# Fused local attention on one core: masks on POOL alone, head sums in one product, late weights in parts, arguments behind projections

## Chip, cores and metric

The kernel runs on one core of a Trainium2 chip. The metric is the device time of one execution in microseconds; less is better.

## What is computed

Two transformer-like layers of three blocks each on x, which is (4, 1024, 512) in float32: a gated linear state space block, cross attention and a stack of linears with tanh; then local attention, cross attention on gathered keys and a gated feed-forward block with FP4 quantisation. A layer norm stands behind each block. The change touches the fourth block, local attention:

```python
g = x @ Wg.T + bg; v = x @ Wv.T + bv             # 16 heads of 32
dot = einsum('bhid,bhjd->bhij', g, g)
nrm = norm(g, axis=-1)
corr = dot / (nrm[..., :, None] * nrm[..., None, :] + 1e-08)
m = (j <= i) & (j >= i - 128)
corr = (corr * m + 1.0) / 2.0
denom = mean(corr, axis=3) + 0.5
fitness = 1.0 / (denom * sum(1.0 / denom, axis=2))
weighted = corr * fitness[..., None]
attn = softmax(weighted * m + (1.0 - m) * NEG)   # NEG = -1e10
out = einsum('bhij,bhjd->bhid', attn, v) @ Wo.T + bo
```

Each query sees itself and the 128 keys before it.

## The kernel before

The program is a row of stages: preparation, the state space block with the products of weights, cross attention with the linears, `local_attention` (L1146), and a last stage for the two remaining attentions' outputs and the feed-forward block. Stages don't overlap.

`local_attention` runs over 4 batches times 4 chunks of 4 heads (16 chunks) times 8 tiles of 128 keys, 128 tiles in all, two per round. A loop over `ROUNDS` is written once per engine, and its order is the order of each engine's queue; semaphores join them. In round s, with p = s + 12 and x = s - 2, the engines work on three ages of tiles at once, held in a ring of 16 buffers `TR`:

- For tiles p and p+1, TensorE makes the arguments (`arguments`, L1426: the two banks 4 and 5, so the arguments of one tile wait until tanh of the tile before has read them), ScalarE takes tanh (L1607), and POOL masks it (`mask_tanh`: L1376 for the keys' own tile of queries, L1381 for the next tile of queries). One round later `gather` (L1432, L1446, L1453) sums tanh over keys with the tiles `GN`.
- Per chunk and half, `sums` (L1525) adds over each head's 32 rows with the block matrix `BO`: four products, each 128 x 32 by 512 columns. ScalarE (`denominator`, `fourth_power`) and VectorE (`inverse`, `share`, `scaled`: L1741 to L1761) make the fitness `GS` of it. In rounds with `sums` the first arguments stand behind the gathers and wait for `denominator` (L1619), which frees bank 4.
- For tiles s and s+1, TensorE makes the scores (`dots`, L1472) in banks 0 to 3, VectorE combines them with the tanh tile (L1714), ScalarE takes the exponential in place (L1612), and POOL masks it (`mask_exp`).
- For tiles x and x+1, `attend` sums values (L1483) and weights (L1486) in bank `PVS`. `mask_exp` masks the own tile only. The unseen corner of the next tile is not zero after the exponential but 1 (its tanh was set to -1, so its exponent is 0), and `unseen` (L1495) takes it back by a product of the values with `UM`, which holds -1 in that corner; the count of it is taken from the sums by the constants `begin` and `begin1`, with which `start_bank` opens the bank.

Beside this the same rounds project the input for batches to come: tile m = p // 4 + 10, in part 0 (here called a g round) the transposes of x (L1537) and the product for g (L1543), in part 1 (a v round) the transposes of unit rows (L1551) and the product for v (L1556). The projections use banks 0 to 3 as well. ScalarE's copies L1641 (x), L1651 (unit rows) and L1656 (v), and VectorE's L1782 (g), empty them; `dots` waits for all of these (L1465 to L1469), and `projections` waits until VectorE has used both scores of its round (L1530). The last projected tile is m = 31, in the rounds up to p = 86; 38 rounds have both scores and a projection. At a batch's end a g round also holds the logarithms (L1662), eight small VectorE steps (L1804 to L1816), and the following v round the transposes L1566 and the copies L1668.

On ScalarE a round is: the square of g, the denominators, tanh(p), exp(s), exp(s+1), tanh(p+1), then the copies of the projection, then `normaliser` (L1636). On TensorE the order at the end of a round is (L1593 to L1599):

```python
if there(x):
    attend(x)
if there(p):
    arguments(p + 1)
projections(*projected(p), s)
if there(x):
    attend(x + 1)
```

SyncE issues the loads of `GN` (L1319), `GT`, `VN` (L1339) and the stores. Once the last tile is projected (p == 98), `weights_after_projections` (L1285) loads the weights of the next stage in one round: `VB`, `Wo` and the feed-forward's down weights, whose four transfers (L1294) go to 32 partitions each.

Of the kernel before, what the change touches and what calls it, by code (L numbers as in the profile page):

```python
# [8 lines left out]
BF16 = mybir.dt.bfloat16  # L9
# [4 lines left out]
P = 128  # L14
B = 4
# [1130 lines left out]
def local_attention(k):  # L1146
# [12 lines left out]
    with ExitStack() as ctx:  # L1159
# [27 lines left out]

        begin, begin1, empty = (sb(n, [P, D], BF16) for n in ("begin", "begin1", "empty"))
# [3 lines left out]
        S0, CR, MC, UM = sb("S0", [P, WIN]), sb("CR", [P, WIN]), sb("MC", [P, P]), sb("UM", [P, P])  # L1192
# [3 lines left out]
        s_zero, s_one, s_bo, s_mc, s_um, s_cm, s_cr, s_con, s_begin = (sem(n) for n in (  # L1196
            "zero", "ones", "block_ones", "causal", "unseen", "count_mm", "count", "constants", "begin"))
# [27 lines left out]
        with k.nc.Block() as block:  # L1225
            @block.sync
            def _(e):
# [57 lines left out]
                def weights_after_projections():  # L1285

                    for s in (s_v, s_gh, s_s2, s_gt):
                        e.wait_ge(s.sem, s.at(NT))
# [14 lines left out]
                for s in ROUNDS:  # L1303
# [39 lines left out]
                e.wait_ge(s_next.sem, s_next.at(32))  # L1343
# [4 lines left out]
            def _(e):  # L1348
# [4 lines left out]
                for t in (begin, begin1, empty):  # L1353
                    e.memset(t[:, :], 0.0).then_inc(s_begin.sem, 1)

                e.memset(MC[:, :], 1.0).then_inc(s_mc.sem, 1)
                e.memset(UM[:, :], -1.0).then_inc(s_um.sem, 1)
# [3 lines left out]
                e.wait_ge(s_um.sem, s_um.at(1))  # L1361
                e.affine_select(out=UM[:, :], in_=UM[:, :], compare_op=ALU.is_ge, fill=0.0, base=-1,
                                pattern=[[1, P]], channel_multiplier=-1).then_inc(s_um.sem, 1)
# [28 lines left out]

# [8 lines left out]
                for s in ROUNDS:  # L1401
# [4 lines left out]
                    if there(s):  # L1406
                        mask_exp(s)
                        mask_exp(s + 1)
# [938 lines left out]
```

## Time and profile before

| | |
|---|---|
| median of 3 runs | 2823.32 us (2823.13 to 2826.96) |
| the profiled execution | 2823.76 us |
| its span, first to last instruction | 2822.0 us |
| mean granted TensorE clock | 0.976 |
| busy: TensorE, VectorE, ScalarE, POOL | 2649.0, 1911.6, 807.9, 799.6 us |
| local attention with scores | about 1057 to 1623 us |
| the last stage | about 1626 to 2822 us |

A row of the timeline gives start, duration, engine, line, operation, the tiles written and read and their shapes, how many instructions were merged, and in brackets the idle time of that engine before them with what ended it. The duration of merged products includes the tail of the last one; how long a group holds TensorE is read from its start to the start of the next. PE is TensorE, ACT is ScalarE, DVE is VectorE, SP is SyncE.

### The profile page before, as it was taken

To read this page: it belongs to the slowest core of one execution; us is meant where nothing else is said; L and a number is where in the kernel's file an instruction comes from. 1 tells how busy PE (TensorE), PEld (TensorE's weight loads), DVE (VectorE), ACT (ScalarE), POOL (GpSimd) and SP (SyncE) were. 2 spreads that over 40 slices of the span, in tenths; PEclk is the share of its full clock that TensorE was granted. 3 is DMA by queue.
4 is the path that set the end of the run, shared out by engine and by line. 5 is a ranking of instruction groups with operands and counts; after the bars stand their busy time and mean duration, and the time that the engine had idled before them with its cause. 6 is when DMAs were issued, how large, how long until landed. Compare 5 with 4: busy or idle time off the path is not lost. (4 is left out here: it accounts for less than half of the span.)

```text
span 2822.0 us, 38888 instructions
## 1 busy us (share of the span) xinstructions
PE 2649.0 (94%) x14094; PEld 1608.6 (57%) x14094; DVE 1911.6 (68%) x3307; ACT 807.9 (29%) x1193; POOL 799.6 (28%) x794
## 2 busy tenths in 40 slices
PE   7999988999998889999997869999999999999996
PEld 3444535555555444555554536777777777777774
DVE  3688403666667336666676748888888888888884
ACT  1111313333332246656576611111111111111110
POOL 1233103555544345554554411111111111111000
PEclk9999989999999999999998979999999999999998
DMA  5344130000000233333335411111111111111111
GB/s 163 120 161 167 60 114 1 1 1 1 1 1 1 65 101 92 91 95 96 94 98 137 147 34 40 43 43 43 43 43 44 43 43 43 43 43 43 40 39 33
DMA packets 219322, 177.04 MB, mean 63 GB/s; under 512 B 38239, under 2 KB 184031, under 8 KB 218110
## 3 DMA queue, kind: packets, MB, share of 16 engines
q1 hardware_dynamic: 182150, 147.85, 17.6%
q10 hardware_dynamic: 36984, 26.71, 3.5%
q8 instruction: 115, 1.88, 0.3%
q14 instruction: 73, 0.60, 0.1%
HBM read 90.51 MB, written 52.43 MB: 51 GB/s over the span
## 5 line engine op out<-in xcount | busy, mean ns | idle before, releaser
L2032 PE MATMUL bank<-tiles,tl_XQT 128*128 128x512 f32 (+1 forms) x768 | 331.3, 575 | 8.6 <-DMA tl_XQT<-tl_QB 5.7
L2047 PE MATMUL bank<-tiles,tl_HT 128*128 128x512 f32 x704 | 317.8, 607 | 19.8 <-DMA tl_HT<-tl_tmp 19.8
L2037 PE MATMUL bank<-tiles,tl_XQT 128*128 128x512 f32 (+1 forms) x768 | 318.0, 557 | 0.0
L2047 PEld LDWEIGHTS bank<-tiles,tl_HT 128*128 128x128 f32 x704 | 225.3, 325 | 96.7 <-issue 29.8
L2032 PEld LDWEIGHTS bank<-tiles,tl_XQT 128*128 128x128 f32 x768 | 232.6, 311 | 74.4 <-issue 16.0
L2037 PEld LDWEIGHTS bank<-tiles,tl_XQT 128*128 128x128 f32 x768 | 236.8, 308 | 65.4
L1376 POOL TENSOR_SCALAR_AFFINE_SELECT tiles<-tiles 128x512 f32<-128x512 f32 x256 | 175.8, 699 | 289.8 <-ACT tiles L1607 259.1
L1985 POOL TENSOR_TENSOR tl_rs<-tl_ve,mhalf 128x1 f32<-128x1 f32 x32 | 17.6, 550 | 594.4 <-DVE tl_ve L2140 594.4
L2081 ACT ACTIVATE tl_HQ<-bank 128x512 f32<-128x512 f32 (+1 forms) x96 | 53.9, 562 | 426.9 <-PE bank L2032 405.5
L1714 DVE SCALAR_TENSOR_TENSOR tiles<-tiles,bank 128x1024 f32<-128x1024 f32 (+1 forms) x128 | 141.8, 1149 | 28.2 <-PE bank L1472 28.0
L1977 POOL TENSOR_TENSOR tl_rs<-tl_ve,mhalf 128x1 f32<-128x1 f32 x32 | 19.9, 622 | 426.0 <-DVE tl_ve L2122 426.0
L1607 ACT ACTIVATE tiles<-bank 128x1024 f32<-128x1024 f32 (+1 forms) x128 | 123.5, 965 | 45.5 <-PE bank L1426 45.4
L1612 ACT ACTIVATE tiles<-tiles 128x1024 f32<-128x1024 f32 (+1 forms) x128 | 124.9, 1000 | 20.0 <-DVE tiles L1714 17.0
L1993 PE MATMUL bank<-home_T,tl_AT 128*128 128x512 f32 x256 | 121.9, 621 | 6.5 <-DMA tl_AT<-attended 6.5
L2115 DVE TENSOR_TENSOR X<-bank,X 128x512 f32<-128x512 f32 x32 | 22.1, 692 | 152.0 <-PE bank L2047 152.0
L960 PE MATMUL bank<-space_T 128*128 128x512 f32 x256 | 121.0, 617 | 2.3 <-DVE X L1108 2.3
L2075 ACT ACTIVATE tl_XT<-bank 128x512 f32<-128x512 f32 x32 | 19.1, 598 | 347.5 <-PE bank L2000 332.6
L1543 PE MATMUL bank<-home_T,tiles 128*128 128x512 f32 x256 | 117.1, 601 | 0.0
L1556 PE MATMUL bank<-home_odd,tiles 128*128 128x512 f32 x256 | 116.7, 599 | 0.0
L1005 PE MATMUL bank<-space_T,space_quant 128*128 128x512 f32 x256 | 115.2, 593 | 1.5 <-ACT space_quant L1062 1.5
L995 PE MATMUL bank<-space_even,space_quant 128*128 128x512 f32 x256 | 115.3, 593 | 1.2 <-ACT space_quant L1057 1.1
L1399 POOL TENSOR_TENSOR la_rn<-la_n,mhalf 128x16 f32<-128x16 f32 x32 | 92.7, 2897 | 50.1 <-DVE la_n L1789 50.1
(289 smaller groups left out, 5025.4 us busy)
## 6 DMA issues: line engine op xcount, KB each, us to landing
tl_HT<-tl_tmp SPq DMA_DIRECT2D x256, 44.0 KB, 2.0
tl_HT<-tl_tmp ACTq DMA_DIRECT2D x256, 44.0 KB, 2.0
fp_weights<-space_quant ACTq DMA_DIRECT2D x33, 256.0 KB, 2.2
X<-in_x SPq DMA_DIRECT2D x8, 1024.0 KB, 11.8
v<-tiles SPq DMA_DIRECT2D x32, 256.0 KB, 2.4
unit_g<-tiles SPq DMA_DIRECT2D x32, 256.0 KB, 2.4
unit_gT<-tiles SPq DMA_DIRECT2D x32, 256.0 KB, 2.8
la_GN<-unit_g SPq DMA_DIRECT2D x128, 64.0 KB, 2.0
```

The source lines that it names most:

```text
L960: mm = e.matmul(bank[turn(s, 0)][:, :], WqT[:, c, m * P:(m + 1) * P], XT[g % 2][:, c, :], start=(c == 0), stop=(c == C - 1))
L995: mm = e.matmul(bank[turn(s, 1)][:, :], AT[:, c, :], WoT[:, c, :], start=(c == 0), stop=(c == C - 1))
L1376: return e.affine_select(out=x[:, :, 0:P], in_=x[:, :, 0:P], compare_op=ALU.is_ge, fill=fill, base=0, pattern=[[0, HC], [1, P]], channel_m ...
L1543: mm = e.matmul(bank[1][:, :], XT[m % 2][:, c, :], WgT[:, c, :], start=(c == 0), stop=(c == C - 1))
L1556: mm = e.matmul(bank[2][:, :], XT[m % 2][:, c, :], WvT[:, c, :], start=(c == 0), stop=(c == C - 1))
L1607: e.activation(TR[p % RING][:, :, 0:cols(t)], four(ARG[:, :])[:, :, 0:cols(t)], ACT.Tanh).then_inc(s_T.sem, 1)
L1612: e.activation(y, y, ACT.Exp).then_inc(s_p.sem, 1)
L1714: e.scalar_tensor_tensor(out=y, in0=y, scalar=1.0, in1=d, op0=ALU.add, op1=ALU.mult).then_inc(s_u.sem, 1)
L1993: mm = e.matmul(bank[LOUT][:, :], AT[n % 2][:, c, :], WoT[:, c, :], start=(c == 0), stop=(c == C - 1))
L2032: mm = e.matmul(bank[(2 * q) % 3][:, 0:w], chunk(XQT[n % 2], c), WgT[q][:, :, c, :], start=(c == 0), stop=(c == C - 1))
L2037: mm = e.matmul(bank[(2 * q + 1) % 3][:, 0:w], chunk(XQT[n % 2], c), WuT[q][:, :, c, :], start=(c == 0), stop=(c == C - 1))
L2047: mm = e.matmul(bank[DOWN][:, :], chunk(HT, q), WdT[:, q, :], start=(q == 0), stop=(q == IC - 1))
```

## The change

1. `mask_exp` masks both halves of the exponentials, as `mask_tanh` does. `unseen`, `UM`, `begin` and `begin1` go; `start_bank` always uses the zeros of `empty`. On POOL the second exponential's mask moves behind the second tanh's.
2. `sums` is one product of 128 x 128 by 512 columns.
3. `weights_after_projections` is called in eleven consecutive rounds, from p = 98 to 118: the down weights in eight parts of 6 or 5 slices to 32 partitions, then `VB`, then `Wo` in two halves.
4. On TensorE `projections` stands ahead of `arguments(p + 1)`.

```diff
+                def weights_after_projections(i):
+
+                    if i == 0:
+                        for s in (s_v, s_gh, s_s2, s_gt):
+                            e.wait_ge(s.sem, s.at(NT))
                     VB, WoT = k.out_weights
-                    e.dma_start(VB, k.SW[:, VO_AT:FOLDED]).then_inc(s_next.sem, 16)
-                    e.dma_start(WoT[:, :, :], chunked(a["L1_attn_Wo_T"])).then_inc(s_next.sem, 16)
-
-                    for j in range(4):
-                        e.dma_start(k.tiles[32 * j:32 * j + 32, DOWN_AT:DOWN_AT + IC * D].rearrange("p (i d) -> p i d", d=D),
-                                    down_rows[32 * IC * j:32 * IC * (j + 1), :].rearrange("(i p) d -> p i d", p=32)).then_inc(k.d_wd, 16)
+                    if i < 8:
+
+                        j, q = i // 2, (0, 6, IC)[i % 2:i % 2 + 2]
+                        at = DOWN_AT + q[0] * D
+                        e.dma_start(k.tiles[32 * j:32 * j + 32, at:at + (q[1] - q[0]) * D].rearrange("p (i d) -> p i d", d=D),
+                                    down_rows[32 * (IC * j + q[0]):32 * (IC * j + q[1]), :].rearrange("(i p) d -> p i d", p=32)).then_inc(k.d_wd, 16)
+                    elif i == 8:
+                        e.dma_start(VB, k.SW[:, VO_AT:FOLDED]).then_inc(s_next.sem, 16)
+                    elif i < 11:
+                        c = 2 * (i - 9)
+                        e.dma_start(WoT[:, c:c + 2, :], chunked(a["L1_attn_Wo_T"])[:, c:c + 2, :]).then_inc(s_next.sem, 16)
...
-                    if p == C * G * (B - 1) + 2:
-                        weights_after_projections()
+                    if p >= C * G * (B - 1) + 2:
+                        weights_after_projections((p - C * G * (B - 1) - 2) // 2)
...
                 def mask_exp(x):
-
                     e.wait_ge(s_p.sem, s_p.at(x + 1))
-                    own_tile(TR[x % RING], 0.0).then_inc(s_pm.sem, 1)
+                    i = own_tile(TR[x % RING], 0.0)
+                    if x % G < G - 1:
+                        i = next_tile(TR[x % RING], 0.0)
+                    i.then_inc(s_pm.sem, 1)
...
                     if there(s):
                         mask_exp(s)
-                        mask_exp(s + 1)
                     if there(p):
                         mask_tanh(p + 1)
+                    if there(s):
+                        mask_exp(s + 1)
...
-                        mm = start_bank(PVS, begin if t else begin1)
+                        mm = start_bank(PVS)
                         if t == 0 and x:
                             mm.then_inc(s_pv.sem, 1)
                         if t:
-                            unseen(x - 1)
                             values(x - 1, P, P).then_inc(s_pv.sem, 1)
...
                     if t % 2 == 0:
-                        unseen(x)
                         values(x, 0, WIN).then_inc(s_pv.sem, 1)
...
-                    for h in range(HC):
-                        q = slice(DH * h, DH * h + DH)
-                        mm = e.matmul(bank[4][q, :], BO[:, q], ZZ[:, half_of(r)], start=True, stop=True)
-                    mm.then_inc(s_S.sem, 1)
+                    e.matmul(bank[4][:, :], BO[:, :], ZZ[:, half_of(r)], start=True, stop=True).then_inc(s_S.sem, 1)
...
                     if there(x):
                         attend(x)
+                    projections(*projected(p), s)
                     if there(p):
                         arguments(p + 1)
-                    projections(*projected(p), s)
                     if there(x):
                         attend(x + 1)
```

TensorE before, from the first arguments of a v round to the next scores:

```order
L1426 MATMUL bank<-la_RR,la_LR 128x512 x2
L1432 MATMUL bank<-la_begin,la_ones 32x512 x4
L1495 MATMUL bank<-la_UM,la_VN 32x128 x4
L1483 MATMUL bank<-tiles,la_VN 32x128 x4
L1486 MATMUL bank<-tiles,ones 32x128 x4
L1495 MATMUL bank<-la_UM,la_VN 32x128 x4
L1483 MATMUL bank<-tiles,la_VN 32x256 x4
L1486 MATMUL bank<-tiles,ones 32x256 x4
L1426 MATMUL bank<-la_RR,la_LR 128x512 x2
L1551 MATMUL bank<-ident,tiles 128x128 x4
L1556 MATMUL bank<-home_odd,tiles 128x512 x4
L1483 MATMUL bank<-tiles,la_VN 32x128 x4
```

TensorE now, the same piece (L1429 is what L1426 was, L1435 was L1432, L1486 and L1489 were L1483 and L1486, L1539 and L1544 were L1551 and L1556):

```order
L1429 MATMUL bank<-la_RR,la_LR 128x512 x2
L1435 MATMUL bank<-la_empty,la_ones 32x512 x4
L1486 MATMUL bank<-tiles,la_VN 32x128 x4
L1489 MATMUL bank<-tiles,ones 32x128 x4
L1486 MATMUL bank<-tiles,la_VN 32x256 x4
L1489 MATMUL bank<-tiles,ones 32x256 x4
L1539 MATMUL bank<-ident,tiles 128x128 x4
L1544 MATMUL bank<-home_odd,tiles 128x512 x4
L1429 MATMUL bank<-la_RR,la_LR 128x512 x2
L1486 MATMUL bank<-tiles,la_VN 32x128 x4
```

The two products against `UM` are gone, and the second pair of argument products stands behind the projection.

SyncE before, where the late weights are issued:

```order
L1231 DMA la_VN<-v 128x128 x2
L1290 DMA home_odd<-folded 128x1536
L1291 DMA home_T<-in_L_attn_Wo_T 128x4x512
L1294 DMA tiles<-fp_weights 32x11x512 x4
L1231 DMA la_GN<-unit_g 128x128 x2
```

SyncE now, from the first part on:

```order
L1230 DMA la_VN<-v 128x128 x2
L1294 DMA tiles<-fp_weights 32x6x512
L1230 DMA la_GN<-unit_g 128x128 x2
L1336 DMA attended<-la_AO 128x256
L1230 DMA la_VN<-v 128x128 x2
L1294 DMA tiles<-fp_weights 32x5x512
```

Each part stands behind the `VN` tiles of its round and ahead of the next round's `GN` tiles.

## Rows read from the trace of the kernel before

**Rows 1.** The stretch with projections and scores: busy time by engine, clock, DMA

```profile
1057.00:1444.00 387.00, 364.23 (x4420) 192.90 (x4420) 248.43 (x466) 237.69 (x330) 204.79 (x237) 1.00 0.33 93
```

**Rows 2.** Timeline of TensorE and ScalarE in a v round

```profile
1250.53 1.06 PE L1525 MATMUL bank<-la_ZZ,la_BO 128*32 128x512 f32 x8
1251.42 0.40 PE L1432 MATMUL bank<-la_empty,la_ones 128*32 128x512 bf16 x4
...
1253.44 0.39 PE L1495 MATMUL bank<-la_UM,la_VN 128*32 128x128 f32 x8
1253.66 0.39 PE L1483 MATMUL bank<-tiles,la_VN 128*32 128x128 f32 x8
...
1255.28 0.39 PE L1426 MATMUL bank<-la_RR,la_LR 32*128 32x512 bf16 x2
1255.60 0.66 PE L1551 MATMUL bank<-ident,tiles 128*128 128x128 f32 x4
1256.09 3.60 PE L1556 MATMUL bank<-home_odd,tiles 128*128 128x512 f32 x8
1259.62 0.43 PE L1483 MATMUL bank<-tiles,la_VN 128*32 128x128 f32 x8
1259.73 0.60 ACT L1656 ACTIVATE tiles<-bank 128x512 f32<-128x512 f32 x1 [2.50 <-PE bank L1556]
1260.69 1.15 PE L1472 MATMUL bank<-la_GS,la_GT 32*128 32x256 f32 x16 [0.42 <-ACT tiles L1656]
```

**Rows 3.** Timeline before the first scores: arguments, tanh, the copy behind it

```profile
1021.29 0.39 PE L1426 MATMUL bank<-la_RR,la_LR 32*128 32x512 bf16 x2 [0.85 <-ACT tiles L1607]
1021.72 1.02 ACT L1607 ACTIVATE tiles<-bank 128x1024 f32<-128x1024 f32 x1 [0.48 <-PE bank L1426]
1022.64 0.59 ACT L1651 ACTIVATE tiles<-bank 128x512 f32<-128x512 f32 x1
```

**Rows 4.** Timeline of a g round's end, then a v round with a narrow second tile

```profile
1269.05 0.16 PEld L1483 LDWEIGHTS bank<-tiles,la_VN 128*32 128x32 f32 x8 [0.76 <-issue]
1270.16 1.15 PE L1472 MATMUL bank<-la_GS,la_GT 32*128 32x256 f32 x16 [0.47 <-issue]
...
1276.85 0.59 ACT L1607 ACTIVATE tiles<-bank 128x512 f32<-128x512 f32 x1
...
1280.63 1.15 PE L1472 MATMUL bank<-la_GS,la_GT 32*128 32x256 f32 x16 [0.42 <-ACT tiles L1656]
```

**Rows 5.** Timeline of the following g round, with the logarithms of a batch

```profile
1286.27 0.59 ACT L1641 ACTIVATE tiles<-bank 128x512 f32<-128x512 f32 x1
...
1288.17 0.31 ACT L1662 ACTIVATE la_ln<-la_nc 128x128 f32<-128x128 f32 x1
...
1291.18 0.94 PE L1472 MATMUL bank<-la_GS,la_GT 32*128 32x256 f32 x16 [1.53 <-issue]
```

**Rows 6.** Late weights: DMA issues (KB each, us to landing), TensorE's wait, scores of every fourth round

```profile
tiles<-fp_weights SPq DMA_DIRECT2D x4, 704.0 KB, 16.3
...
1483.82 1.15 PE L1472 MATMUL bank<-la_GS,la_GT 32*128 32x256 f32 x16 [0.65 <-DVE la_GS L1761]
...
1507.08 1.08 PE L1453 MATMUL bank<-tiles,la_GN 128*32 128x256 f32 x8 [15.29 <-DMA la_GN<-unit_g]
...
1524.90 1.15 PE L1472 MATMUL bank<-la_GS,la_GT 32*128 32x256 f32 x16 [0.65 <-DVE la_GS L1761]
...
1549.07 1.15 PE L1472 MATMUL bank<-la_GS,la_GT 32*128 32x256 f32 x16 [0.65 <-DVE la_GS L1761]
```

**Rows 7.** Behind the projections: second tanh, head sums; POOL's selects, ns min/median/max

```profile
1553.63 1.00 ACT L1607 ACTIVATE tiles<-bank 128x1024 f32<-128x1024 f32 x1
...
1555.10 1.06 PE L1525 MATMUL bank<-la_ZZ,la_BO 128*32 128x512 f32 x8
...
L1376 POOL TENSOR_SCALAR_AFFINE_SELECT tiles<-tiles x256: 628/634/1130, 1014.6 to 1615.0; 128x512 f32<-128x512 f32 x128
```

**Rows 8.** Timeline of TensorE near the stage's end: scores after a gap

```profile
1596.29 1.62 PE L1472 MATMUL bank<-la_GS,la_GT 32*128 32x256 f32 x16 [2.44 <-DVE la_GS L1761]
```

More of the change, by code:

```diff
@@ L1185, in local_attention @@
         ones16 = sb("ones16", [P, DH], BF16)
-        begin, begin1, empty = (sb(n, [P, D], BF16) for n in ("begin", "begin1", "empty"))
+        empty = sb("empty", [P, D], BF16)
         ZZ, UU = sb("ZZ", [P, T]), sb("UU", [P, D])
@@ L1191, in local_attention @@
         SQ = [sb(f"SQ{n}", [P, WIN]) for n in range(2)]
-        S0, CR, MC, UM = sb("S0", [P, WIN]), sb("CR", [P, WIN]), sb("MC", [P, P]), sb("UM", [P, P])
+        S0, CR, MC = sb("S0", [P, WIN]), sb("CR", [P, WIN]), sb("MC", [P, P])
         BO, half = sb("BO", [P, P]), sb("half", [P, 1])
@@ L1195, in local_attention @@
         S2, S, S4, rS = sb("S2", [P, 2]), sb("S", [P, 1]), sb("S4", [P, 1]), sb("rS", [P, 1])
-        s_zero, s_one, s_bo, s_mc, s_um, s_cm, s_cr, s_con, s_begin = (sem(n) for n in (
-            "zero", "ones", "block_ones", "causal", "unseen", "count_mm", "count", "constants", "begin"))
+        s_zero, s_one, s_bo, s_mc, s_cm, s_cr, s_con, s_begin = (sem(n) for n in (
+            "zero", "ones", "block_ones", "causal", "count_mm", "count", "constants", "begin"))
         d_row = [sem(f"load_rows{n}") for n in range(2)]
@@ L1352, in _ @@
                 e.memset(ones16[:, :], 1.0).then_inc(s_begin.sem, 1)
-                for t in (begin, begin1, empty):
-                    e.memset(t[:, :], 0.0).then_inc(s_begin.sem, 1)
+                e.memset(empty[:, :], 0.0).then_inc(s_begin.sem, 1)
                 e.memset(MC[:, :], 1.0).then_inc(s_mc.sem, 1)
-                e.memset(UM[:, :], -1.0).then_inc(s_um.sem, 1)
                 e.wait_ge(s_mc.sem, s_mc.at(1))
@@ L1428, in arguments, with start_bank @@
                     mm.then_inc(s_arg.sem, 1)
-                def start_bank(n, src):
+                def start_bank(n):
                     for h in range(HC):
-                        mm = e.matmul(bank[n][DH * h:DH * h + DH, :], ones16[:, :], src[:, :], start=True, stop=False)
+                        mm = e.matmul(bank[n][DH * h:DH * h + DH, :], ones16[:, :], empty[:, :], start=True, stop=False)
                     return mm
@@ L1438, in gather @@
                         e.wait_ge(s_z.sem, s_z.at(2 * n))
-                        start_bank(WB, empty)
+                        start_bank(WB)
                     if t == HG:
                         e.wait_ge(s_z.sem, s_z.at(2 * n + 1))
-                        start_bank(WB, empty)
+                        start_bank(WB)
                         for h in range(HC):
@@ L1488, in values @@
                     return mm
-                def unseen(x):
-                    c = ((x + 1) % 2) * P
-                    for h in range(HC):
-                        q = slice(DH * h, DH * h + DH)
-                        e.matmul(bank[PVS][q, c:c + P], VN[x % TILES][:, q], UM[:, :], start=False, stop=False)
                 def attend(x):
@@ L1522, in sums @@
                         e.wait_ge(s_bo.sem, s_bo.at(3))
-                    for h in range(HC):
-                        q = slice(DH * h, DH * h + DH)
-                        mm = e.matmul(bank[4][q, :], BO[:, q], ZZ[:, half_of(r)], start=True, stop=True)
-                    mm.then_inc(s_S.sem, 1)
+                    e.matmul(bank[4][:, :], BO[:, :], ZZ[:, half_of(r)], start=True, stop=True).then_inc(s_S.sem, 1)
                 def projections(m, part, s):
@@ L1821, in constants @@
                     e.reciprocal(MC[:, :], bank[PVS][:, 0:P]).then_inc(s_con.sem, 1)
-                    e.wait_ge(s_begin.sem, s_begin.at(4))
-                    e.tensor_scalar(begin[0:1, WIN:WIN + P], bank[PVS][0:1, 0:P], 1.0, -1.0, ALU.subtract, ALU.mult)
-                    e.tensor_scalar(begin[0:1, WIN + P:2 * WIN], bank[PVS][0:1, 0:P], 1.0, -1.0, ALU.subtract, ALU.mult).then_inc(s_begin.sem, 1)
-                    e.tensor_scalar(begin1[0:1, WIN + P:2 * WIN], bank[PVS][0:1, 0:P], 1.0, -1.0, ALU.subtract, ALU.mult).then_inc(s_begin.sem, 1)
                     e.wait_ge(s_con.sem, s_con.at(2))
@@ L2042, in down @@
                     if n == 0:
-                        e.wait_ge(k.d_wd, 64)
+                        e.wait_ge(k.d_wd, 128)
                     e.wait_ge(s_a6.sem, s_a6.at(n))
```

11 lines of the change are left out of this document (1 added, 10 removed).

## Prediction

> **What bounds the kernel now.** I first read the page's slices: TensorE is busy 9 tenths or more nearly throughout, except in the slices around 1440 to 1620 us, inside local attention. The chain of waits starts behind this stage and says nothing of it, so I went by stretches. From 1057 to 1444 us, while projections run beside attention, TensorE is busy 364 of 387 us at full clock [rows 1]. A microsecond of TensorE is there a microsecond of the kernel, unless somebody else takes over. Then I read the timeline of single rounds, to see which wait ends last in each.
>
> One round handles two tiles. In the projection stretch two kinds alternate. A **v round** ends with the product of values; its block of L1556 is over where L1483 starts, at 1259.62. Behind it ScalarE copies the bank (L1656), and TensorE's next scores (L1472) start 1.07 us after the product's end, and 0.96 us after the copy's start [rows 2]. So the copy already binds: the scores want the bank that the copy empties. A **g round** ends the same way, 1.11 us from product to scores [rows 4]. The tanh of the second tile is done long before, since its arguments (L1426) stand ahead of the projection [rows 2].
>
> Behind the projections four rounds take 24.17 us (1524.90 to 1549.07), but the four in which the late weights load take 41.08 (1483.82 to 1524.90) [rows 6]. In them L1294 puts four transfers of 704 KB, which land 16.3 us later, into the one queue that also carries the GN tiles, and TensorE stands still for 15.29 us until such a tile arrives.
>
> The profiled execution took 2823.76 us, its span is 2822.0, the median of three runs 2823.32. The sum is made against 2823.8, which is 0.4 us above that median.
>
> **Part 1: the arguments behind the projections.** This is the dearest part, and it is a loss. ScalarE's order is not changed: tanh(p), two exponentials, tanh(p+1), then the copies of the projection. The diff puts arguments(p+1) on TensorE behind the projection, so tanh(p+1) starts only then, and the copies wait behind it on ScalarE. With T the end of the projection product, rows of the time before the first scores give each step: arguments to tanh 0.43, tanh to the copy behind it 0.92 [rows 3]. In a v round there follow the copy of unit rows, about 0.50 (an estimate: it is 0.59 long, and the tanh of 1.02 was followed after 0.92), and 0.96 from L1656 to the scores [rows 2]. Scores at T + 2.81, where they were at T + 1.07: 1.74 later. T itself is earlier by the arguments that left (0.32, from 1255.28 to 1255.60) and by two products against UM that the other part removes (0.22 each, 1253.44 to 1253.66; together 0.43). Net **+0.99 us**. In every second v round the second tile is half as wide: its tanh takes 0.59 instead of 1.02 [rows 4], only one UM product stands there (0.22) and the arguments are half as long (0.21), so +0.88. In a g round the copy of x stands directly behind the tanh: 0.43 + 0.92 + 0.59 + 0.36 = 2.30 against 1.11 [rows 3, 4], less 0.75: **+0.44**.
>
> 38 rounds have a projection and scores, 19 of each kind. Two g rounds also hold the logarithms, whose table load and eight small VectorE steps come behind the copy of x: 1.90 us from that copy to the logarithm and 3.01 from there to the next scores [rows 5]. Now these run beside the product; behind it, the scores come at T + 6.26. T is 8.36 − 0.75 = 7.61 us into the round [rows 2, 4], so 13.87 us instead of 10.55 (1280.63 to 1291.18) [rows 4, 5]: +3.3 each. Two v rounds hold two more copies of 0.5 behind the product: +1.5 each. Sum: 17 × 0.44 + 2 × 3.3 + 7 × 0.99 + 10 × 0.88 + 2 × 1.5 = 32.8. The six rounds before the first scores: tanh(p+1) now holds up the next arguments instead of tanh(p) the second; +0.4 each at most, 2 in all. The 5 us gaps of the two logarithm rounds should cost clock: after a gap of 2.44 us the same scores took 1.62 us where they take 1.15 [rows 8]. I take 1.5 us each, 3. Part 1 with the UM products of these rounds: **+38**.
>
> What is behind the waiting scores: the two steps scores(s), scores(s+1) on VectorE, then the exponentials; all shift with them and none was the bound of these rounds. On POOL the mask of tanh(p+1) and the inverse norm come later too, but the inverse norm is wanted only late in the next round.
>
> **Part 2: masks on POOL, UM products gone.** 112 groups of products go, 0.22 us each, 24 us of TensorE. In projection rounds they are counted above. In the 26 rounds behind them they are worth little: of four rounds (24.17 us) only in the first does TensorE hold the others up. Its second tanh starts 4.56 us in and ends at about 5.58, the head sums that need its bank start at 6.03 [rows 7]: 0.4 us can be won, the rest of the four rounds hangs on tanh, exponentials and the fitness chain. 6.5 × 0.41 = **−2.7**. POOL takes 112 selects more; the median of one is 0.63, the longest 1.13 [rows 7]. A round then has up to eight of them, 5.1 of 6.0 us, and their results are wanted one round later. I cost that at nothing; the cover is this microsecond. SBUF — State Buffer, section "SBUF: two separate sides", in the Trainium skill, says that a VectorE operation with two SBUF inputs and a reading GpSimd operation exclude each other for the whole instruction, whichever starts first. The spread of the selects agrees. By that rule the fitness chain, which binds one late round in four, could lose up to a select's length each time, an estimate of some 4 us in all.
>
> **Part 3: head sums in one product.** Four narrow products of 512 columns took 0.89 us together (1250.53 to 1251.42) [rows 2]. One full product of 512 columns takes a quarter of the L1556 block, (1259.62 − 1256.09) / 4 = 0.88 [rows 2]. So nothing is won. TensorEngine Tiling, section "Key Properties", in the Trainium skill, says that a change of tiling mode drains the array, and one more change stands here; by an estimate from that rule the part would lose in each of its 32 uses. The rows show a change of shape from L1426 to L1551 at about 0.1 (0.32 for a product of 0.21). I take 0.07 × 32 = **+2**; bounds 0 and +6.
>
> **Part 4: late weights in parts.** Four rounds of 41.08 against 24.16: the stall with its slow clock costs 16.9 us. A part is 0.4 MB (VB 0.8, a half of Wo 0.5) behind the VN tiles of its round. 2.8 MB landed in 16.3 us [rows 6], so a part takes about 2.3 us, VB 4.5. The next GN tiles are issued some 3 us later, and have another 3 in hand. **−16.9**; if every part still held up its round by 1 us, −6.
>
> The zeroed and filled constants at the start lie under the first projections: 0.
>
> **Sum:** +38 + 2 − 2.7 − 16.9 = +20.4. **Predicted 2844 us.**
>
> **Rivals.** *All gains real, no new wait.* If tanh(p+1) did not hold the scores, because ScalarE's copies were done within 1.82 us of T (the 1.07 of now and the 0.75 that T wins), the projection rounds would gain 0.43 each: −8 to −16 there, −19.6 behind, about 2790. For it: TensorE now waits for tanh(p) in some rounds. Against it: 2.81 us of fixed steps stand in ScalarE's queue, a full microsecond too many. It decides at 1.82. Chance 0.07, and 0.12 for a cheaper form, in which half of the loss is hidden: about 2827.
>
> *Clock lost in every v round.* The new gap ahead of the scores is about 1.8 us. Gaps of 1.53 [rows 5] left the scores' speed alone, one of 2.44 did not [rows 8]. If 1.8 is enough, each of 19 rounds loses up to 1.7: +30, 2874. Chance 0.1.
>
> *POOL becomes the bound.* If selects stretch beside VectorE to 0.9 us on average, between median and longest, eight take 7.2 us against rounds of 6.0. The gathers wait for the tanh masks from 0.75 us a select on; +0.5 to 1 in 26 rounds gives 2857 to 2870. The median speaks against it. Chance 0.1.
>
> My own case has 0.61.
>
> **How the numbers follow.** A measurement can tell 0.2%, 5.6 us, from no change. Faster than that: the first rival and a few of its cheaper form, 0.1. Within it: most of the cheaper form, 0.1. Slower: 0.8. The forecast alone spans 2836 to 2854 (half or one and a half of the logarithm rounds and of the stall's relief). The range must take in the POOL case and the near edge of the cheaper form: 2826 to 2870.
>
> **What would show it.** Right: scores (L1472 of before) wait for ScalarE's copies by about 1.8 us in v and 1.3 in g rounds, tanh has an idle time of some 4 us ahead of its second tile, a cycle of four projection rounds lasts 43.1 instead of 40.4, and the logarithm rounds nearly 14. The wait for GN is gone, and four rounds behind the projections take 23.8. Wrong: projection rounds under 9.5 us, a DMA wait of several us at the new parts, POOL without idle time, or slow products in the v rounds.

## The result, and the profile after

| | before | after |
|---|---|---|
| median | 2823.38 us of 4 runs (2823.13 to 2826.96) | 2858.48 us of 4 runs (2856.91 to 2858.99) |
| profiled execution, its span | 2823.76, 2822.0 us | 2858.96, 2857.2 us |
| mean granted TensorE clock | 0.976 | 0.971 |

The ratio is 1.012 (95% interval 1.0103 to 1.0138): slower, by 35 us. 2844 was forecast, with 2826 to 2870 as the range. The direction and the range hold; the size is 14.5 us short. One of the fifteen runs of the kernel before in the second group of experiments took 8473.08 us, for a reason that isn't known, and no ratio below uses it.

The changed lines keep their form and have new numbers: the scores L1475 (was 1472), arguments L1429 (1426), tanh L1595 (1607), the copies L1629 (x, was 1641), L1639 (unit rows, 1651), L1644 (v, 1656) and L1656 (YT, 1668), the v product L1544 (1556), the head sums L1514 (1525), `scores` on VectorE L1702 (1714).

I begin with the same stretch of time as in [rows 1]. The columns are stretch, length, busy time of TensorE, its weight loads, VectorE, ScalarE, POOL, then granted clock and DMA.

```profile
1057.00:1444.00 387.00, 327.82 (x3313) 166.66 (x3313) 218.30 (x409) 206.79 (x290) 209.38 (x266) 0.94 0.29 81
```

TensorE was busy 364 of these 387 us at full clock; now it is busy 328, with a clock of 0.94. Both losses that follow are in this one line: it waits, and it runs slower. (The stretch is the same, the work in it is not: fewer rounds fit.) POOL's busy time rose only from 204.8 to 209.4, though it masks more in each round.

The end of a full v round in the timeline of TensorE and ScalarE, with the head sums at its start, answers to [rows 2]:

```profile
1277.08 1.12 PE L1514 MATMUL bank<-la_ZZ,la_BO 128*128 128x512 f32 x2
1278.14 0.40 PE L1435 MATMUL bank<-la_empty,la_ones 128*32 128x512 bf16 x4
...
1281.92 3.60 PE L1544 MATMUL bank<-home_odd,tiles 128*128 128x512 f32 x8
1285.45 0.39 PE L1429 MATMUL bank<-la_RR,la_LR 32*128 32x512 bf16 x2
1285.88 1.02 ACT L1595 ACTIVATE tiles<-bank 128x1024 f32<-128x1024 f32 x1 [3.49 <-PE bank L1429]
1286.80 0.59 ACT L1639 ACTIVATE tiles<-bank 128x512 f32<-128x512 f32 x1
1287.28 0.60 ACT L1644 ACTIVATE tiles<-bank 128x512 f32<-128x512 f32 x1
1288.24 1.15 PE L1475 MATMUL bank<-la_GS,la_GT 32*128 32x256 f32 x16 [1.83 <-ACT tiles L1644]
```

The product ends at 1285.45 (T). The arguments follow it, tanh starts 0.43 later, the copy of unit rows 0.92 after that, the copy of v another 0.48, and the scores 0.96 behind its start: T + 2.79, where 2.81 was worked out. The scores wait 1.83 us for the copy.

The next two microseconds were not in the forecast's sum. The same stretch by windows of 2 us, columns as above:

```profile
1286.00:1288.00 2.00, 0.41 (x16) 0.14 (x8) 0.00 (x0) 2.00 (x4) 0.95 (x2) 1.00 0.11 33
1288.00:1290.00 2.00, 1.76 (x24) 1.09 (x28) 0.98 (x2) 0.57 (x2) 2.00 (x3) 0.85 0.59 166
1290.00:1292.00 2.00, 2.00 (x36) 1.43 (x32) 2.00 (x3) 1.92 (x3) 2.00 (x2) 0.50 0.40 113
1292.00:1294.00 2.00, 2.00 (x29) 1.18 (x22) 2.00 (x6) 0.89 (x1) 2.00 (x4) 0.79 0.36 114
```

The granted clock falls to 0.50, which is 1.2 instead of 2.4 GHz, and is back after some 3 us. All products in between take longer: the g round that follows lasts 11.38 us (1288.24 to 1299.62). The g round behind a narrow v round, whose wait is 1.40, lasts 9.68 (1266.54 to 1276.22); before, the two kinds took 9.47 and 9.37. The wait of 1.83 comes seven times in this execution, and the g round behind it loses time each time: six take 11.4 us, and the seventh, which has less to project, takes 10.06 with a clock of 0.50 in its third and fourth microsecond. But the wait ahead of the very first scores, 2.40 us, and the next one, 1.76, left the clock at 1.00.

Next the waits between 1057 and 1660 us (total, times, longest):

```profile
POOL tiles L1376 <- ACT tiles L1595: 231.9, 85, 10.4
ACT tiles L1595 <- PE bank L1429: 175.9, 68, 5.5
...
PE bank L1475 <- ACT tiles L1644: 29.3, 18, 2.4
...
PE bank L1475 <- ACT tiles L1629: 18.8, 16, 1.8
...
PE bank L1475 <- issue: 11.3, 3, 5.5
...
PE bank L1475 <- ACT la_YT L1656: 7.2, 3, 2.6
```

ScalarE waits for arguments 68 times. TensorE waits for ScalarE's copies ahead of the scores, 55 us by the lines on L1644, L1629 and L1656 together, and 11 more in the logarithm rounds ("issue"). POOL itself waits for tanh, as a follower would; whether it is one the first experiment decides.

A logarithm round and the v round behind it in the timeline, answering to [rows 5]:

```profile
1131.27 0.39 PE L1429 MATMUL bank<-la_RR,la_LR 32*128 32x512 bf16 x2
1131.70 1.02 ACT L1595 ACTIVATE tiles<-bank 128x1024 f32<-128x1024 f32 x1 [3.41 <-PE bank L1429]
1132.62 0.59 ACT L1629 ACTIVATE tiles<-bank 128x512 f32<-128x512 f32 x1
...
1134.52 0.31 ACT L1650 ACTIVATE la_ln<-la_nc 128x128 f32<-128x128 f32 x1
...
1137.77 1.66 PE L1475 MATMUL bank<-la_GS,la_GT 32*128 32x256 f32 x16 [5.54 <-issue]
...
1153.53 2.09 PE L1475 MATMUL bank<-la_GS,la_GT 32*128 32x256 f32 x16 [2.55 <-ACT la_YT L1656]
```

The copy, the logarithm and VectorE's small steps now begin behind the product. The scores, at 1123.63 a round earlier, come at 1137.77 after 5.54 us of idle TensorE: the round takes 14.14 (13.87 was worked out). The next scores come at 1153.53, 15.76 us later, partly at half clock; and behind their own wait of 2.55 us the next g round takes 12.73 us, again partly at half clock.

Behind the projections the late weights (DMA issues: number, KB each, us to landing) and the scores of every fourth round answer to [rows 6]:

```profile
tiles<-fp_weights SPq DMA_DIRECT2D x4, 384.0 KB, 4.5
...
tiles<-fp_weights SPq DMA_DIRECT2D x4, 320.0 KB, 4.0
```

```profile
1539.44 1.15 PE L1475 MATMUL bank<-la_GS,la_GT 32*128 32x256 f32 x16 [1.09 <-DVE la_GS L1749]
...
1563.48 1.15 PE L1475 MATMUL bank<-la_GS,la_GT 32*128 32x256 f32 x16 [1.09 <-DVE la_GS L1749]
```

No GN tile is waited for; the four rounds with the first parts take 24.03 us (1515.41 to 1539.44) and the next four 24.04.

So the spans of the profiled executions differ by 35.2 us as follows: +0.9 up to the first scores; +54.8 in the 40 rounds behind them (1057.16 to 1459.68 before, 1058.06 to 1515.41 now: 402.5 and 457.35 us); −17.1 in eight late rounds (65.22 against 48.07); +0.5 in the rest of the scores; −3.9 behind the last scores, which start at 1610.88 and 1649.95. That last piece lies between 1207 and 1212 us in the kernels of this study, whatever they change, and I ascribe it to no edit.

### The profile page after: what moved, and what is told of

It is laid out like the page before. It is cut to its first block and busy times, and to the rows that moved or that the text cites. A ratio compares the mean times of both kernels' runs of the same rounds, so it can differ in the third digit from the quotient of the medians.

```text
span 2857.2 us, 36840 instructions
## 1 busy us (share of the span) xinstructions
PE 2648.9 (93%) x13006; PEld 1592.8 (56%) x13006; DVE 1915.8 (67%) x3304; ACT 806.0 (28%) x1193; POOL 859.7 (30%) x902
## 5 line engine op out<-in xcount | busy, mean ns | idle before, releaser
L1376 POOL TENSOR_SCALAR_AFFINE_SELECT tiles<-tiles 128x512 f32<-128x512 f32 x256 | 174.4, 684 | 268.8 <-ACT tiles L1595 252.9
L1595 ACT ACTIVATE tiles<-bank 128x1024 f32<-128x1024 f32 (+1 forms) x128 | 124.1, 969 | 199.6 <-PE bank L1429 198.9
L1702 DVE SCALAR_TENSOR_TENSOR tiles<-tiles,bank 128x1024 f32<-128x1024 f32 (+1 forms) x128 | 141.8, 1149 | 34.7 <-PE bank L1475 34.5
L1381 POOL TENSOR_SCALAR_AFFINE_SELECT tiles<-tiles 128x512 f32<-128x512 f32 x224 | 151.6, 677 | 0.0
L1475 PE MATMUL bank<-la_GS,la_GT 32*128 32x256 f32 (+1 forms) x1024 | 74.5, 406 | 74.1 <-ACT tiles L1644 29.3
L1600 ACT ACTIVATE tiles<-tiles 128x1024 f32<-128x1024 f32 (+1 forms) x128 | 124.8, 1000 | 19.0 <-DVE tiles L1702 15.9
```

Of the source, the lines that this page charges most:

```text
L1376: return e.affine_select(out=x[:, :, 0:P], in_=x[:, :, 0:P], compare_op=ALU.is_ge, fill=fill, base=0, pattern=[[0, HC], [1, P]], channel_m ...
L1381: return e.affine_select(out=x[:, :, P:WIN], in_=x[:, :, P:WIN], compare_op=ALU.is_ge, fill=fill, base=0, pattern=[[0, HC], [-1, P]], chan ...
L1595: e.activation(TR[p % RING][:, :, 0:cols(t)], four(ARG[:, :])[:, :, 0:cols(t)], ACT.Tanh).then_inc(s_T.sem, 1)
L1600: e.activation(y, y, ACT.Exp).then_inc(s_p.sem, 1)
L1702: e.scalar_tensor_tensor(out=y, in0=y, scalar=1.0, in1=d, op0=ALU.add, op1=ALU.mult).then_inc(s_u.sem, 1)
```

## The experiments

Theory A: the order on TensorE makes tanh(p+1), and behind it the copies, late. Theory B: the masks on POOL cost the time. Theory C, an addition to A: the wait of 1.83 us takes the clock. Each kernel is compared with runs of the kernel before on the same chip, whose medians were 2823.39, 2822.79 and 2823.40 us in the three groups. Stretches given as "40 rounds" run from the first scores to those 40 rounds later; lengths of rounds and waits are of the profiled execution of each kernel.

### The old order on TensorE

```diff
-                    projections(*projected(p), s)
                     if there(p):
                         arguments(p + 1)
+                    projections(*projected(p), s)
```

> The changed kernel with arguments(p+1) ahead of the projections again, everything else of the change kept. Theory A (the order on TensorE costs the time, because tanh(p+1) and behind it ScalarE's copies hold up the scores): the four projection rounds fall from 44.5 us to 40.4 less 4 x 0.43 = 38.7 to 39.5, and the total to 2790 to 2800 us. Theory B (the masks that moved to POOL cost it): 2840 us or more, scores still late.

Measured: 2796.62 us (2793.78 to 2797.78), ratio 0.9902 (0.9886 to 0.9919). The scores in TensorE's timeline:

```profile
1238.04 1.15 PE L1475 MATMUL bank<-la_GS,la_GT 32*128 32x256 f32 x16 [0.42 <-ACT tiles L1644]
1246.97 0.94 PE L1475 MATMUL bank<-la_GS,la_GT 32*128 32x256 f32 x16 [0.36 <-issue]
1257.58 1.15 PE L1475 MATMUL bank<-la_GS,la_GT 32*128 32x256 f32 x16 [0.42 <-ACT tiles L1644]
...
1277.01 1.15 PE L1475 MATMUL bank<-la_GS,la_GT 32*128 32x256 f32 x16 [0.42 <-ACT tiles L1644]
```

Four rounds take 38.97 us (1238.04 to 1277.01), and the wait for the copy is 0.42 again. POOL masks as much here as in the changed kernel, and the time is 62 us less. Theory A stands, B falls.

### The new order alone

```diff
                     if there(x):
                         attend(x)
+                    projections(*projected(p), s)
                     if there(p):
                         arguments(p + 1)
-                    projections(*projected(p), s)
```

> The kernel before with nothing but arguments(p+1) put behind the projections. Theory A: it loses what the changed kernel lost in its projection rounds (52 + 2.5 us) and also what the products against UM gave back there (38 x 0.43 = 16 us), less the 24 dearer head sums of that stretch (about 3.5 us): about +67, 2885 to 2895 us. Theory B: at most 2840 us.

Measured: 2878.13 us (2874.29 to 2879.36), ratio 1.0192 (1.0177 to 1.0207): 54.7 us lost by two lines that change places. It is 7 us less than the lower end of what I expected. The timeline shows one reason, a clock that is lost less often:

```profile
1244.73 2.09 PE L1472 MATMUL bank<-la_GS,la_GT 32*128 32x256 f32 x16 [1.86 <-ACT tiles L1656]
...
1247.18 1.32 PE L1453 MATMUL bank<-tiles,la_GN 128*32 128x256 f32 x16
...
1290.52 1.15 PE L1472 MATMUL bank<-la_GS,la_GT 32*128 32x256 f32 x16 [1.83 <-ACT tiles L1656]
...
1291.80 0.86 PE L1453 MATMUL bank<-tiles,la_GN 128*32 128x256 f32 x16
```

and its windows behind the two waits:

```profile
1246.00:1248.00 2.00, 2.00 (x18) 0.66 (x18) 1.12 (x1) 0.71 (x1) 1.59 (x1) 0.50 0.60 165
1292.00:1294.00 2.00, 2.00 (x62) 1.62 (x57) 2.00 (x3) 1.96 (x2) 2.00 (x3) 1.00 0.62 171
```

The wait is nearly the same, 1.86 and 1.83 us, but only the first of the two lost the clock. Of the six ordinary g rounds behind a full v round, three last 11.8 us and three 10.2, in turn; the seventh, shorter one kept the clock too. In the changed kernel all six last 11.4, where 9.8 is the length at full clock. So the loss from the wait itself is there in both kernels, and that from the clock is hit or miss. Longer waits are no surer: ahead of the scores near the stage's end this kernel waits 2.44 us, just as the kernel before does in [rows 8], and here they take 1.15 us, there 1.62.

### The wait filled

```diff
+                    m, part = projected(p)
...
                     if there(x):
                         attend(x + 1)
+                    if part == 1 and tile(m) and there(x) and m < NT - 1:
+                        for i in range(3):
+                            for h in range(HC):
+                                e.matmul(bank[WB][DH * h:DH * h + DH, :], ones16[:, :], empty[:, :], start=False, stop=False)
```

> The changed kernel with twelve products of ones by zeros (1.2 us of TensorE) added to the open gather bank in each v round, behind the last values, so that they fill most of the wait for ScalarE's copies and change no number. Theory C (the wait of 1.83 us takes TensorE's clock, which makes the g round behind a full v round 1.5 us longer): that g round falls from 11.39 to about 9.8 us, the granted clock there returns to 1.0, and the total falls by 12 to 18 us to 2841 to 2847 us. Rival (the slow products there have another cause, such as POOL's longer masks): the same 2858 us or more.

Measured: 2840.07 us (2836.31 to 2841.49), ratio 1.0058 (1.0043 to 1.0073), 18.4 us less than the changed kernel, by added work. Its timeline:

```profile
1280.31 0.83 PE L1592 MATMUL bank<-la_empty,la_ones 128*32 128x512 bf16 x12
1282.32 1.15 PE L1475 MATMUL bank<-la_GS,la_GT 32*128 32x256 f32 x16 [1.18 <-ACT tiles L1649]
```

and the window behind the wait:

```profile
1284.00:1286.00 2.00, 2.00 (x53) 1.25 (x42) 2.00 (x3) 1.88 (x3) 2.00 (x2) 1.00 0.53 149
```

Twelve products took 0.8 us, not the 1.2 I had thought, and the scores still start when the copy lets them; the v round stays at 12.02 us. But the wait is 1.18, the clock stays at 1.00, and the g round behind falls from 11.4 to 9.78 us. Theory C holds. The expected 12 to 18 us were just passed: 16.6 of it lies in the 40 rounds (457.35 to 440.78), and 15.9 of that in the 17 g rounds. Not every slow round was cured: of the two g rounds that follow a logarithm round and its v round, one still takes 11.40 us, the other 9.78.

### ScalarE's order follows

```diff
-                    if there(p):
-                        tanh(p + 1)
                     if part == 0:
...
                         if b is not None:
                             y_transposed(b)
+                    if there(p):
+                        tanh(p + 1)
```

> The changed kernel with TensorE's new order kept, but on ScalarE the copies of the projection ahead of tanh(p+1). Theory A: the copies start 0.1 us behind their products as in the kernel before, the scores follow 1.07 to 1.11 us behind them, and what stays is that tanh(p+1), now last, is over 0 to 0.5 us after the next arguments could start; total 2805 to 2825 us. Theory B: 2840 us or more.

Measured: 2786.94 us (2784.75 to 2790.24), ratio 0.9872 (0.9858 to 0.9887), well under the expected range. The end of a full v round in its timeline of TensorE and ScalarE:

```profile
1207.31 3.60 PE L1544 MATMUL bank<-home_odd,tiles 128*128 128x512 f32 x8
1210.85 0.39 PE L1429 MATMUL bank<-la_RR,la_LR 32*128 32x512 bf16 x2
1210.95 0.60 ACT L1644 ACTIVATE tiles<-bank 128x512 f32<-128x512 f32 x1 [2.67 <-PE bank L1544]
...
1211.44 1.02 ACT L1595 ACTIVATE tiles<-bank 128x1024 f32<-128x1024 f32 x1
1211.91 1.15 PE L1475 MATMUL bank<-la_GS,la_GT 32*128 32x256 f32 x16
1212.89 0.38 PE L1429 MATMUL bank<-la_RR,la_LR 32*128 32x512 bf16 x2
```

The copy starts 0.10 us behind the product, and the scores 0.96 behind the copy, as before. Now the arguments and the last values stand between product and scores and fill that time, so the row of the scores has no wait. tanh(p+1) is over at 1212.46, before the next arguments want to start (1212.89): it holds up nobody. I had expected 0 to 0.5 us lost there and no gain from the filled wait. Four rounds take 38.55 us (1192.58 to 1231.13). The logarithm rounds gain too:

```profile
1118.35 0.58 ACT L1629 ACTIVATE tiles<-bank 128x512 f32<-128x512 f32 x1
1118.94 1.28 ACT L1650 ACT_TABLE_LOAD   x1
1120.24 0.31 ACT L1650 ACTIVATE la_ln<-la_nc 128x128 f32<-128x128 f32 x1
```

The copy and the logarithm lie beside the product again; the round takes 10.18 us, and the wait ahead of the scores is 1.19.

One round pays for this order, which no expectation counted. Behind the last product of values stands one more logarithm with its table load. It now goes ahead of tanh(p+1), and the head sums wait for that tanh:

```profile
1435.23 1.95 PE L1514 MATMUL bank<-la_ZZ,la_BO 128*128 128x512 f32 x2 [3.31 <-ACT tiles L1595]
```

The clock falls to 0.50 behind the wait, and the last of the 40 rounds takes 12.60 us; it was 10.66 in the kernel before.

### Single parts on the kernel before

The masks alone: `mask_exp` for both tiles and POOL's new order, no `unseen`, `UM`, `begin`, `begin1`:

```diff
-                            unseen(x - 1)
...
-                        unseen(x)
...
-                    own_tile(TR[x % RING], 0.0).then_inc(s_pm.sem, 1)
+                    i = own_tile(TR[x % RING], 0.0)
+                    if x % G < G - 1:
+                        i = next_tile(TR[x % RING], 0.0)
+                    i.then_inc(s_pm.sem, 1)
```

> The kernel before with only its second part: products against UM gone, POOL masks both tiles of the exponentials. Theory A (the step of the prediction): 0.43 us less for each of 38 projection rounds and 0.12 to 0.41 for each four late rounds, so 16 to 19 us less, 2804 to 2808 us. Theory B (POOL's longer masks hold others up): 2815 us or more.

Measured: 2812.50 us (2808.21 to 2814.99), ratio 0.9963 (0.9949 to 0.9978): 10.3 us less, a miss. The four ordinary rounds gained what the prediction had worked out for them, 40.33 to 38.81; the 0.43 for every round that I expected here was too much, since narrow v rounds gain only 0.22. More went in the logarithm rounds, as TensorE's timeline shows:

```profile
1283.74 1.04 PE L1469 MATMUL bank<-la_GS,la_GT 32*128 32x256 f32 x16 [2.41 <-issue]
```

There the logarithm chain ends last, and a faster TensorE only waits longer, 2.41 us instead of 1.53. These rounds grew from 10.55 to 10.99 us. One of the two v rounds behind them kept 12.23 us; the other went to 13.20, with a clock of 0.61 in the 2 us behind the wait. In the old_order kernel both lost it (14.16 and 12.74, against 12.22). The last of the 40 rounds grew as well, from 10.66 to 11.78, and the late rounds gave next to nothing. The trace is of one of the two fastest of the five executions (2808.34 us); what made three others 4 to 7 us longer, it can't show.

The late weights alone (the diff's `weights_after_projections` and its call):

```diff
-                    if p == C * G * (B - 1) + 2:
-                        weights_after_projections()
+                    if p >= C * G * (B - 1) + 2:
+                        weights_after_projections((p - C * G * (B - 1) - 2) // 2)
```

> The kernel before with only the late weights loaded in parts: the stall of 15.3 us on a GN tile is gone, 17 us less, 2806 to 2807 us. If the parts held up their own rounds, 2810 us or more.

Measured: 2805.30 us (2803.94 to 2806.98), ratio 0.9939 (0.9926 to 0.9952): 17.5 us less, as expected.

The head sums alone:

```diff
-                    for h in range(HC):
-                        q = slice(DH * h, DH * h + DH)
-                        mm = e.matmul(bank[4][q, :], BO[:, q], ZZ[:, half_of(r)], start=True, stop=True)
-                    mm.then_inc(s_S.sem, 1)
+                    e.matmul(bank[4][:, :], BO[:, :], ZZ[:, half_of(r)], start=True, stop=True).then_inc(s_S.sem, 1)
```

> The kernel before with only the head sums in one full product. By the prediction 0.07 us each, +2, 2826 us. By the rows of the changed kernel (first arguments 1.02 to 1.06 us behind the start of the sums, where it was 0.89) 0.13 to 0.17 each in 32 uses: +4 to +5.5, 2827.5 to 2829 us.

Measured: 2824.85 us (2822.20 to 2827.26), ratio 1.0007 (0.9998 to 1.0016): +2.0, between −0.6 and +4.5. Its timeline:

```profile
1250.07 1.13 PE L1523 MATMUL bank<-la_ZZ,la_BO 128*128 128x512 f32 x2
1251.12 0.40 PE L1432 MATMUL bank<-la_empty,la_ones 128*32 128x512 bf16 x4
```

The next product starts 1.05 us behind the sums, where it was 0.89. The rounds with sums (they are v rounds) grew by 0.11 us where the second tile is narrow (10.47 to 10.58) and by 0.03 in the others (11.02 to 11.05). So part of the 0.16 is absorbed further on, and by the rounds the prediction's 2 was nearer than the 4 to 5.5 that I read out of the changed kernel. The interval alone excludes neither no loss at all nor 4.

### All gains with the old order and the old sums

The diff of the change without its last part, and with `sums` in four products.

> The changed kernel with the old order and the head sums in four products, so the kernel before with masks on POOL and weights in parts. If the parts add up, it is under old_order (2796.6) by what the one product costs, 4 to 5.5 us: 2791 to 2793 us. If the one product costs only what the prediction took, 2794 to 2795 us.

Measured: 2795.59 us (2793.71 to 2796.80), ratio 0.9903 (0.9889 to 0.9918). That is 1.0 us under old_order, less than the two intervals can tell apart. The parts add up: 17.5 and 10.3 us from 2823 give 2795. That is the second of the two cases, the cheap product.

### The fourth corner of the two orders

The edits of old_order and copies_first together: the old order on TensorE, ScalarE's copies ahead of tanh(p+1).

> The changed kernel with the old order on TensorE, and ScalarE's copies ahead of tanh(p+1): the fourth corner of the two orders. If ScalarE's order alone makes copies_first fast, it comes to 2787 us. If the two orders belong together (the arguments and last values behind the product fill TensorE's wait for the copy, which the old order leaves open for 0.4 us), it stays at old_order's 2797 us, or up to 7 us above, since tanh(p+1) may then end after the next arguments could start: 2796 to 2804 us.

Measured: 2800.39 us (2796.89 to 2802.60), ratio 0.9919 (0.9906 to 0.9933). With the rest of the change in place, the four corners are:

| | tanh(p+1) ahead of the copies | copies ahead of tanh(p+1) |
|---|---|---|
| arguments ahead of projections | 2796.6 | 2800.4 |
| arguments behind projections | 2858.5 | 2786.9 |

Neither order is good or bad by itself. Alone on TensorE the new order loses 62 us. Together the two gain 10. Alone on ScalarE it gains nothing: the medians are 4 us apart the wrong way, but the intervals of the two ratios overlap, and the traces don't show where 4 us would lie. With the copies first, tanh(p+1) waits for them although its arguments are there, and the g round behind a full v round takes 9.39 us instead of 9.04 to 9.14; the logarithm rounds and the v rounds behind them are shorter in return, and the 40 rounds take 395.1 us against 395.9.

### Both orders, nothing else

```diff
+                    projections(*projected(p), s)
                     if there(p):
                         arguments(p + 1)
-                    projections(*projected(p), s)
...
-                    if there(p):
-                        tanh(p + 1)
...
+                    if there(p):
+                        tanh(p + 1)
```

> The kernel before with the arguments behind the projections on TensorE and the copies ahead of tanh(p+1) on ScalarE, and nothing else. If the order that lost 55 us in reorder_only is a gain once ScalarE's order goes with it: copies_first (36.5 us less) without the parts measured alone (17.5 and 10.3 less, 2 more), so about 11 us less, 2809 to 2815 us. If it needs the removed products to pay: 2820 us or more.

Measured: 2816.19 us (2813.95 to 2819.63), ratio 0.9978 (0.9969 to 0.9987): 7.2 us less, 1 us above the expected range. The gain does not need the removed products. Here the last of the 40 rounds, with its logarithm, takes 13.92 us instead of 10.66: the head sums wait 3.29 us for tanh(p+1), and the clock is 0.50 behind the wait. So 3.3 us of gain are given back in this one round.

### The fastest with four sums

The edit of copies_first, and `sums` in four products.

> The fastest so far, copies_first, with the head sums in four products again: 1 to 3 us under its 2786.9, so 2784 to 2786 us; the g rounds with sums 0.1 us shorter.

Measured: 2786.31 us (2785.06 to 2789.39), ratio 0.9871 (0.9858 to 0.9885). The narrow rounds with sums do take 10.04 instead of 10.14 us (v rounds; I had written g), but of the 1 to 3 us only 0.6 shows, which no interval here can tell from nothing. Both versions are 36 to 37 us faster than the kernel before and 72 faster than the changed one.

## Why the prediction was right, and where it was short

**What bounds the kernel.** Right. TensorE's time was the kernel's time in the projection stretch, and ScalarE's copy already ended last ahead of the scores. That is why a delay of tanh went through to the end undamped.

**Part 1, the chain T + 2.81 and its relatives.** Right to a few hundredths in v rounds and to 0.3 us in the others: a full v round lasts 12.02 us (12.01 worked out, 11.02 before), a narrow one 11.34 (11.35), the g round behind a narrow one 9.68 (9.81), a logarithm round 14.14 (13.87). With the clock kept in the ordinary rounds, in the keep_warm kernel, the 40 rounds take 38.3 us more than before. The prediction's terms for them are 32.8, 3 for the clock behind the logarithm rounds, and about 1.6 for sums. One round stood in no term: the one behind the last projection, where TensorE waits once more for the copies YT (L1656). It takes 13.61 us instead of 10.66, and 12.03 in keep_warm.

**The step that failed** is "Clock lost in every v round", which had a chance of 0.1, together with the bound that part 1 took over from it: that only the two logarithm rounds cost clock, 3 us. The forecast put nothing on a wait of 1.83 us, because 1.53 had left the speed alone and 2.44 had not. The 1.83 us of the full v rounds took the clock each time in the profiled execution, and filling the wait gave back 18.4 us in the median. The rival had its own error: it counted 19 rounds, but the narrow v rounds wait only 1.40 and keep the clock. At its own price of up to 1.7, nine full v rounds would have come to 15 us, not 30. Forecast plus that corrected rival is 2859, beside the measured 2858.5. That it comes so near is partly luck: against the forecast's terms the 40 rounds cost 17 us more (15 of it in the 17 g rounds, 22.2 for 7.5, and nearly 3 in the forgotten round) and the late rounds some 3 more, while the ramp cost 1 less and the piece behind the last scores was 4 shorter.

**Part 2.** Its price for ordinary rounds was right (1.51 us for four rounds by the rows, 1.52 measured). Behind the projections it was wrong. "0.4 us can be won, the rest of the four rounds hangs on" other things: the first of the four did fall from 4.96 to 4.53 us, but the third grew from 5.55 to 5.94 us in the changed kernel and from 5.55 to 5.79 with the masks alone. In both, the scores after it wait 1.09 us for the end of the fitness chain instead of 0.65: TensorE's gain is spent waiting for VectorE. Four ordinary late rounds fell only from 24.17 to 24.04 us, and the last twelve before the gap of [rows 8] take 71.37 instead of 71.39. −2.7 became about 0. In the changed kernel the arguments, now behind the scores' wait in `projections` (L1518), also wait for VectorE there; the two are not separated. POOL at nothing was right: the copies_first kernel keeps POOL busy for longer than the changed one, 865.3 against 859.7 us, and its TensorE waits 0.7 us for POOL in the whole projection stretch. By the rule that the prediction took from the Trainium skill (SBUF — State Buffer, section "SBUF: two separate sides"), the additional selects could have stretched the fitness chain by some 4 us. The traces don't show it for the chain: over 72 us of late rounds of the kernel with the masks alone the chain's steps average 685, 692 and 687 ns, before 686, 692 and 686, and the scaling at its end takes 1.22 and 0.85 us in turn in the ordinary rounds of all three kernels. One short addition outside the chain, `la_AO` by `la_CR`, did grow in these rounds, from 0.29 to 0.48 us with the masks alone and to 0.40 in the changed kernel. It starts beside a select of POOL in those two kernels and behind one before; that fits the rule, but was not tested.

**Part 3.** +2, measured +2.0, with an interval that takes in 0 and 4. The row of sums_only shows 0.16 us more at the place itself, more than the 0.07 taken. TensorEngine Tiling (Array Packing), section "Key Properties", in the Trainium skill, says that a change of mode drains the array, and the row agrees with that in direction. By the medians less than half of it reached the end.

**Part 4.** −16.9, and −17.0 in the trace (41.08 to 24.04), −17.5 alone. The landing of a part was put too low, 4.0 to 4.5 us for about 2.3, and it still fits between two loads of GN tiles.

**The other rivals.** "All gains real" was the kernel with the old order, at 2797; as a rival to this change it needed ScalarE's copies within 1.82 us of T, and they took 2.79. The copies_first kernel, whose copies start 0.10 us behind T, is on the other side of its turning point, and shows the way there that I hadn't looked at: to change the other engine's order. "POOL becomes the bound" was wrong.

**What would show it.** The waits of 1.8 us, the 3.5 us of idle ScalarE ahead of the second tanh (4 was given), the logarithm rounds at 14 and the missing wait for GN all came. The cycle of four rounds is 44.4 us instead of 43.1, and the four late rounds 24.04 instead of 23.8. "Slow products in the v rounds" was listed as a sign against me, and slow products came, in the g rounds behind them.

## What to carry to other kernels

An order on one engine's queue is only half of a schedule: when work moves behind another piece on TensorE, ask what on ScalarE stands behind the step that consumes it, and move that too. The same two lines cost 62 us with one order of ScalarE and gained 13.5 with the other. When a wait gets longer, price it twice, once for its length and once for the clock behind it; and read from the trace which lengths have been harmless, without trusting the space between the harmless and the harmful one.

## What the runs showed of the hardware

- A wait of 1.83 us on TensorE in every fourth round brought the granted clock to 0.50 for some 3 us, seven times of seven in the changed kernel, and one of 1.83 or 1.86 only three times of seven in the kernel with the order alone. Waits of 1.40 in the narrow v rounds never did, and neither did the 2.40 ahead of the first scores. The length of the wait alone does not decide.
- Useless products gave time back: twelve products of ones by zeros, 0.8 us in each v round and off the critical path, saved 18 us.
- A gain made the clock worse: with less work on TensorE ahead of the logarithm rounds' wait, it grew from 1.53 to 2.4 us, and the v round behind it rose from 12.22 to as much as 14.16 us; in the three kernels with masks on POOL and the old order it stayed at 12.23 once and rose five times.
- A full 128 x 128 product in float32 of 512 columns between narrow ones took 1.05 us to the next start, four narrow ones 0.89.
